# Second attention in two-step units with merged diagonal steps and VectorE masks; products issued in two parts in both attentions

## The reference

```python
xn = _layernorm(x)
s = _L0_attn_ref(xn, ...)              # full attention: softmax(q k / sqrt(8)) v, output matrix, residual
g = _silu(_L0_ffn_ref(xn, W_fc, W_proj))   # square(relu), then 5 steps of a spiking neuron
x = x + s * g
xn = _layernorm(x)
s = _L1_attn_ref(xn, ...)              # causal attention with a bias that is linear in the key's position
g = _silu(_L1_ffn_ref(xn, ...))        # 3 cycles of a small coupling network
x = x + s * g
```

```python
attn = attn + alibi
attn = jnp.where(causal, attn, jnp.finfo(x.dtype).min)
p = jax.nn.softmax(attn, axis=-1)
```

## Time and profile before

| | us |
|---|---|
| device time, median of 3 runs | 1046.53 (1045.78 to 1047.62) |
| device time of the profiled execution | 1043.26 |
| its span | 1041.5 |
| first attention, first to last exponential | 69.3 to 592.8 |
| middle | 597.6 to 681.0 |
| second attention, first to last exponential | 685.1 to 1026.7 |
| TensorE busy | 883.8 (85%) |
| ScalarE busy | 858.6 (82%) |
| VectorE busy | 439.0 (42%) |
| GpSimd busy | 122.6 (12%) |

### The profile page before, as it was taken

The page is one execution under the profiler, slowest core; times in us unless marked ns, Lnnn a source line. Parts: engine busy times, 40 slices in busy tenths (PEclk is TensorE's granted clock), DMA queues, the critical chain, the costliest instruction groups (busy, mean ns, idle before and its releaser), DMA issues. The chain is left out here.

```text
span 1041.5 us, 18319 instructions
## 1 busy us (share of the span) xinstructions
PE 883.8 (85%) x7078; PEld 337.8 (32%) x7078; DVE 439.0 (42%) x915; ACT 858.6 (82%) x1017; POOL 122.6 (12%) x135
## 2 busy tenths in 40 slices
PE   2757998799998999989999788768888899889886
PEld 1322333233333333323333242323333333334332
DVE  7522163443656426563265777802212411222222
ACT  5748999999999999999999756567878878887883
POOL 1001020130202302023020210000011002002001
PEclk9869999999999999999999999869999999999999
DMA  5862020100202002020000160100202202112000
GB/s 159 272 224 29 1 65 2 63 4 1 86 21 71 36 1 86 21 80 26 1 21 21 42 185 0 41 1 2 65 18 70 66 1 84 31 33 84 0 0 21
DMA packets 31950, 52.97 MB, mean 51 GB/s; under 512 B 5512, under 2 KB 16392, under 8 KB 31880
## 3 DMA queue, kind: packets, MB, share of 16 engines
q1 hardware_dynamic: 31880, 52.01, 16.1%
HBM read 31.29 MB, written 20.71 MB: 50 GB/s over the span
## 5 line engine op out<-in xcount | busy, mean ns | idle before, releaser
L921 ACT ACTIVATE a_probs<-a_sc 128x1024 f32<-128x1024 f32 x512 | 483.5, 1030 | 46.8 <-PE a_sc L1110 46.4
L1784 ACT ACTIVATE a_probs<-a_sc 128x1024 f32<-128x1024 f32 (+3 forms) x384 | 283.5, 819 | 55.3 <-PE a_sc L1912 50.3
L1124 PE MATMUL a_o<-a_probs,vt 128*18 128x512 f32 x2048 | 244.7, 595 | 0.0
L1110 PE MATMUL a_sc<-q_st,k_st 32*128 32x512 f32 x1024 | 130.6, 496 | 55.4 <-ACT a_probs L921 48.2
L1926 PE MATMUL a_o<-a_probs,a_v_st 128*16 128x512 f32 (+3 forms) x1536 | 163.2, 498 | 6.7 <-DVE a_o_sb L1857 6.7
L1110 PEld LDWEIGHTS a_sc<-q_st,k_st 32*128 32x128 f32 x1024 | 53.1, 183 | 215.2 <-ACT a_probs L921 201.2
L1906 PE MATMUL a_sc<-q_st,k_st 32*128 32x512 f32 (+3 forms) x768 | 87.7, 443 | 36.9 <-ACT a_probs L1784 30.2
L1857 DVE COPY a_o_sb<-a_o 128x512 f32<-128x512 f32 x32 | 22.1, 691 | 158.7 <-PE a_o L1926 158.7
L1906 PEld LDWEIGHTS a_sc<-q_st,k_st 32*128 32x128 f32 x768 | 39.8, 185 | 141.7 <-issue 98.4
L1124 PEld LDWEIGHTS a_o<-a_probs,vt 128*18 128x18 f32 x2048 | 47.4, 97 | 111.3 <-issue 72.0
L948 POOL TENSOR_TENSOR a_hidden<-a_hidden 128x512 f32<-128x512 f32 x32 | 38.4, 1200 | 158.5 <-DVE a_hidden L1048 158.5
(11 more groups left out here) (234 smaller groups left out, 827.1 us busy)
## 6 DMA issues: line engine op xcount, KB each, us to landing
q_st<-q_hl SPq DMA_DIRECT2D x48, 256.0 KB
k_st<-k_hl SPq DMA_DIRECT2D x48, 256.0 KB
q_hl<-parts SPq DMA_DIRECT2D x12, 512.0 KB, 3.4
k_hl<-parts SPq DMA_DIRECT2D x12, 512.0 KB, 4.0
q_hl<-p_parts SPq DMA_DIRECT2D x4, 512.0 KB, 3.9
k_hl<-p_parts SPq DMA_DIRECT2D x4, 512.0 KB, 4.7
out_dram<-x SPq DMA_DIRECT2D x8, 256.0 KB, 2.3
x<-in_L_attn_x_dram SPq DMA_DIRECT2D x3, 512.0 KB, 5.8
```

The lines of the kernel that those rows point to most:

```text
L921: nc.scalar.activation(probs[t % RING][:, 2 * pair:2 * pair + 2, :], scores[unit % SLOTS][:, :, :], ACT.Exp).then_inc(expd, 1)
L1110: ins = nc.tensor.matmul(scores[(2 * t + i // 2) % SLOTS][:, i % 2, :], k_st[part, g, kt * P:(kt + 1) * P], q_st[part, g, qh * HALF:(qh + ...
L1124: ins = nc.tensor.matmul(o_ps[32 * h:32 * h + 2 * W9, :], vt[b % 2][:, kt, gp, h, W9 * gs:W9 * gs + 2 * W9], probs[t % RING][:, h, :], sta ...
L1784: nc.scalar.activation(probs[j % PR][:, 2 * pair:2 * pair + 2, 0:HALF - q0], scores[unit % SC][:, :, 0:HALF - q0], ACT.Exp).then_inc(exp_d ...
```

## The change

- First attention: product(t) takes a range of columns. For an odd step the last 256 queries are issued one pair later, between score(2p) and the side piece; the even step and the first 256 queries of the odd one stay after score(2p+1).
- Second attention, new in the manner of the first: steps in pairs, `LAG1` 2, `RING` 4, two groups share one bank `o_ps` (18 columns of values per head), the same 32x32 transposes on VectorE at each of the now 4 ends of a sequence. Diagonal blocks are three steps instead of four: width 512, widths 384 and 128 side by side in one 512-wide step, width 256. So 40 steps a sequence, 160 in all, 320 exponentials. Products of odd steps are shared out as in the first attention (a merged step by its two blocks).
- Masks: group 0 (`STEEP` is 1) keeps the mask matmuls. The other three groups' probabilities are masked after the exponential on VectorE: min with 3e38 and times a 0/1 triangle, in place, 4 heads x 128 columns each; the product waits for it. A merged step has two masks.
- `turn_out` and `keep` are gone from the middle; the same transposes are side pieces `z` of the second attention with a copy on VectorE. Its gate is tanh on ScalarE and one VectorE operation. The last half's `mix` is done in two `tail` pieces with VectorE instead of GpSimd.
- The output matrix of layer 1 is loaded as `wo_x1` in eight small DMAs, issued between those of `wo_x` and that of `bo`. Two tiny activations load Gelu's and Exp's tables at the start and end of the middle. Values of two sequences are spread at once (`spread`).
- The second attention clears its semaphores at its end (`sem.wiped`).

```diff
-                by_slot = a["L0_attn_w_out"].rearrange("(g s j d) c -> s j d g c", g=2, s=2, j=G)
-                for s2 in range(2):
-                    for j in range(G):
-                        at = 32 * j + W9 * s2
-                        sp.dma_start(s["wo_x"][at:at + D, :, :], by_slot[s2, j]).then_inc(s["wo_in"], 16)
+                for name, slots, wait in (("L0_attn_w_out", s["wo_x"], s["wo_in"]), ("L1_attn_Wo", s["wo_x1"], s["w1_in"])):
+                    by_slot = a[name].rearrange("(g s j d) c -> s j d g c", g=2, s=2, j=G)
+                    for s2 in range(2):
+                        for j in range(G):
+                            at = 32 * j + W9 * s2
+                            sp.dma_start(slots[at:at + D, :, :], by_slot[s2, j]).then_inc(wait, 16)
...
-                        dve.wait_ge(s["w1_in"], 16 * 7)
+                        dve.wait_ge(s["w1_in"], 16 * (2 * G + 6))
+                        nc.vector.tensor_scalar_mul(s["wo_x1"][:, :, :], s["wo_x1"][:, :, :], 0.5)
+                        nc.vector.tensor_scalar_mul(s["bo"][:, 1, :], s["bo"][:, 1, :], 0.5)
...
-                def product(t):
+                def product(t, c0, c1):
                     b, gp, qh, gs, kt = place(t)
                     opens, closes = gs == 0 and kt == 0, gs == 1 and kt == BT - 1
-                    pe.wait_ge(expd, 2 * t + 2)
-                    if opens and t > 0:
-                        pe.wait_ge(o_free, t // STEP_END)
-                    if b > 0 and t % PER == 0:
-                        pe.wait_ge(side_in, fill_index("v0", b, 1) + 1)
+                    if c0 == 0:
+                        pe.wait_ge(expd, 2 * t + 2)
+                        if opens and t > 0:
+                            pe.wait_ge(o_free, t // STEP_END)
+                        if b > 0 and t % PER == 0:
+                            pe.wait_ge(side_in, fill_index("v0", b, 1) + 1)
                     for h in range(G):
-                        ins = nc.tensor.matmul(o_ps[32 * h:32 * h + 2 * W9, :], vt[b % 2][:, kt, gp, h, W9 * gs:W9 * gs + 2 * W9],
-                                               probs[t % RING][:, h, :], start=opens, stop=closes, tile_position=(0, 32 * h))
-                    ins.then_inc(pv_done, 1)
+                        ins = nc.tensor.matmul(o_ps[32 * h:32 * h + 2 * W9, c0:c1], vt[b % 2][:, kt, gp, h, W9 * gs:W9 * gs + 2 * W9],
+                                               probs[t % RING][:, h, c0:c1], start=opens, stop=closes and c1 == HALF, tile_position=(0, 32 * h))
+                    if c1 == HALF:
+                        ins.then_inc(pv_done, 1)
 
...
+                    if 0 <= 2 * pair - 1 - LAG < S:
+                        product(2 * pair - 1 - LAG, CUT, HALF)
                     for one in pieces_at(pair):
                         piece_of(*one)
                     if 2 * pair < S:
                         score(2 * pair + 1)
-                    for t in (2 * pair - LAG, 2 * pair + 1 - LAG):
-                        if 0 <= t < S:
-                            product(t)
+                    if 0 <= 2 * pair - LAG < S:
+                        product(2 * pair - LAG, 0, HALF)
+                        product(2 * pair + 1 - LAG, 0, CUT)
         sem.wiped()
...
+                nc.scalar.activation(warm[:, :], scalars[:, 0:2], ACT.Gelu)
...
-                keep(0, pa[:, 0:2, :])
                 couple(ROUNDS - 1, 0)
                 couple(ROUNDS - 1, 1)
-                keep(1, pb[:, 0:2, :])
-                keep(2, pb[:, 2:4, :])
-                keep(3, pa[:, 0:2, :])
+                nc.scalar.activation(warm[:, :], half_b[:, :], ACT.Exp)
 
...
+LAG1 = 2
+STEEP = 1
+
+
+def causal_steps():
+
+    steps = []
+    for gp in range(2):
+        for qh in range(2):
+            own = HT * qh
+            for gs in range(2):
+                blocks = [([(kt, 0, 0, HALF)], ()) for kt in range(own)]
+                blocks.append(([(own, 0, 0, HALF)], (0,)))
+                blocks.append(([(own + 1, P, 0, 3 * P), (own + 3, 3 * P, 3 * P, P)], (0, 3)))
+                blocks.append(([(own + 2, 2 * P, 0, 2 * P)], (0,)))
+                for n, (pieces, masked) in enumerate(blocks):
+                    opens, closes = gs == 0 and n == 0, gs == 1 and n == len(blocks) - 1
+                    steps.append((gp, qh, gs, pieces, masked, opens, closes))
+    return steps
+
+
...
+        if 0 < b < B:
+            fill("mix", b - 1, 1, 3, 4)
+        if b < B:
+            fill("z", b, 0, 5)
+            fill("z", b, 1, 6)
+            fill("mix", b, 0, 16, 17)
+        else:
+            fill("tail", b - 1, 0, 1)
+            fill("tail", b - 1, 1, 2)
...
+                for t in range(S):
+                    b, r = divmod(t, PER1)
+                    if t >= RING:
+                        act.wait_ge(pv_done, t - RING + 1)
+                    for pair in range(2):
+                        unit = 2 * t + pair
+                        act.wait_ge(scored, unit + 1)
+                        nc.scalar.activation(probs[t % RING][:, 2 * pair:2 * pair + 2, 0:width(t)],
+                                             scores[unit % SLOTS][:, :, 0:width(t)], ACT.Exp).then_inc(expd, 1)
...
+                def lift(e):
+                    b, k = divmod(e, ENDS)
+                    dve.wait_ge(pv_done, PER1 * b + closing[k] + 1)
+                    nc.vector.transpose(turn[e % 2][:, :], o_ps[:, :]).then_inc(o_free, 1)
+
+                def settle(e):
+                    t = turn[e % 2]
+                    used = t[:, :].rearrange("p (n r) -> p n r", r=32)[:, :, 0:2 * W9].rearrange("p n (s r) -> p n s r", r=W9)
+                    dve.wait_ge(o_free, e + 1)
+                    ends.after(nc.vector.reciprocal(recip[:, :, :], used[:, :, :, D]))
+                    ends.after(nc.vector.tensor_tensor(
+                        used, used, recip[:, :, :].rearrange("p n (s o) -> p n s o", o=1).broadcast_to([P, HALF // 32, 2, W9]), ALU.mult))
+                    nc.vector.transpose(on[e % ENDS][:, :], t[:, :]).then_inc(on_rdy, 1)
+
+                def mask(t):
+                    step = plan[t % PER1]
+                    if not late_mask(step):
+                        return
+                    dve.wait_ge(expd, 2 * t + 2)
+                    keep = tri[:, :].rearrange("p (o q) -> p o q", o=1).broadcast_to([P, G, P])
+                    for n in step[4]:
+                        part = probs[t % RING][:, :, n * P:(n + 1) * P]
+                        ins = nc.vector.scalar_tensor_tensor(part, part, LARGEST, keep, ALU.min, ALU.mult)
+                    ins.then_inc(masked, 1)
+
+                def gate(b, hf):
...
+                e = 0
+                for pair in range(LAST):
+                    b, r = divmod(pair, PER1 // 2)
+                    ending = e < B * ENDS and 2 * pair - LAG1 == PER1 * (e // ENDS) + closing[e % ENDS] + 1
+                    if ending:
+                        lift(e)
+                    if 0 <= 2 * pair - 1 < S:
+                        mask(2 * pair - 1)
+                    for n, kind, at, hf, piece, pieces in pieces_at(pair):
+                        if piece == pieces - 1 and kind != "tail":
+                            evacuate(n, kind, at, hf)
+                    if 2 * pair < S:
+                        mask(2 * pair)
+                    if ending:
+                        settle(e)
+                        e += 1
+                    for n, kind, at, hf, piece, pieces in pieces_at(pair):
+                        if kind == "tail":
+                            evacuate(n, kind, at, hf)
+                    for hf in range(2):
+                        if b < B and r == GATE_AT[hf]:
+                            gate(b, hf)
 
             @block.tensor
...
+                    for n, (kt, q0, at, w) in enumerate(pieces):
...
+                        if early:
+                            for i in range(G):
+                                ins = nc.tensor.matmul(banks[i][:, early[n] * P:(early[n] + 1) * P], s["ident_bf"][:, :],
+                                                       s["mask_kq"][:, :], start=False, stop=True)
+                                if i % 2 == 1 and n == len(pieces) - 1:
+                                    ins.then_inc(scored, 1)
...
+                def shares(t):
+
+                    pieces = plan[t % PER1][3]
+                    if t % 2 == 0:
+                        return pieces, []
+                    if len(pieces) == 2:
+                        return pieces[:1], pieces[1:]
+                    kt, q0, at, w = pieces[0]
+                    if w < HALF:
+                        return pieces, []
+                    return [(kt, 0, 0, CUT)], [(kt, CUT, CUT, HALF - CUT)]
+
+                def product(t, share):
+                    b, r = divmod(t, PER1)
+                    gp, qh, gs, _, _, opens, closes = plan[r]
+                    pieces = shares(t)[share]
```

(23 more changed lines are left out.)

406 lines of the change are left out of this document (163 added, 243 removed).

## The result

The changed kernel takes 982.41 us (median of 4 runs, 980.99 to 982.99) where the kernel before took 1046.88 on the same chip: ratio 0.9383, 95% interval 0.9367 to 0.9399. It is 64 us faster, 18 us more than the 46.7 of the forecast.

What follows compares the result with a forecast made beforehand. The prediction took ScalarE as the fullest engine, with its idle time nearly all ended by TensorE's scores. Gains of 12.5 (first attention), 27.5 (second), 3.1 (middle) and 3.6 (tail) sum to 46.7: 1046.53 to about 1000 us, range 974 to 1024.

Steps and rivals of the forecast that it cites:

- First attention, products in parts: First attention: splitting products evens TensorE's halves, pairs fall from 4.05 us to 3.95, 3.91 or 3.80; 18.5 us, less 1.7 for tanh.
- The lower case of a half product free of its start: First attention: if the half product pays no starting cost, heavy pairs take 3.83 us and the gain is 30.
- ScalarE alone binds: Rival, both attentions: TensorE's extra starts overlap, first attention at 3.80 a pair, second with 20 us idle; 970 us, chance 0.14.
- The cost at the start: Start of first attention: eight wo_x1 loads ahead of bo make VectorE, then TensorE, wait longer; 4.3 us lost.
- Exponentials: Second attention: 64 pairs of widths 384 and 128 become one full exponential each; 9.2 us gained.
- Idle time of the second attention: Second attention: ScalarE's idle time falls from 54.7 to 36.4 us, summed part by part; 18.3 us gained.
- late TensorE in the diagonal units: Second attention: halves of pairs around diagonal steps overrun, 0.8 us for each of 8 halves-of-heads; 6.4 us of idle time left.
- masks of group 0: Second attention: mask matmuls of 0.33 us, 8 a sequence, where TensorE is already late; 10.6 us of idle time left.
- Masks on VectorE: Second attention: masks moved to VectorE cost nothing, hidden because the product is due about 2.5 us after its exponential.
- The rival of small waits: Rival, second attention: VectorE finishes masks late, 0.3 us on each of 72 masked steps, 22 us; 1022 us, chance 0.19.
- The clock: Rival, second attention: fewer matmuls let TensorE's clock fall, full pairs take 5.1 us instead of 3.77; slower, chance 0.04.
- Middle and tail: Middle without turn_out and keep ends with VectorE, 3.1 us gained; stretch after the last exponential falls 12.0 to 8.4, 3.6 gained.

Runs made afterwards that it cites:

- experiment 7: The changed kernel with a second operation of the mask's kind and size, to spare tiles, ahead of each VectorE mask: 1004.46 us, ratio 0.9603.
- experiment 5: The changed kernel with whole products in the second attention, order and lag kept: 994.12 us, ratio 0.9502.
- experiment 6: The changed kernel with the diagonal steps unmerged (512, 384, 256, 128 columns), masks on VectorE, mixing pieces at units 19 and 20: 1062.26 us, ratio 1.0169.
- experiment 9: The changed kernel with unmerged diagonal steps (512, 384, 256, 128) and all masks on TensorE: 1069.06 us, ratio 1.0207.
- experiment 10: The changed kernel with unmerged diagonal steps in the order 512, 128, 384, 256, masks on VectorE: 1024.43 us, ratio 0.9794.
- experiment 12: The changed kernel with unmerged diagonal steps, all masks on TensorE, and one whole product behind each score: 1041.2 us, ratio 0.9974.
- experiment 2: The changed kernel with whole products in the first attention: 1004.26 us, ratio 0.9607.
- experiment 3: The changed kernel with the loads of bo ahead of the eight of wo_x1: 977.36 us, ratio 0.9348.
- experiment 4: The changed kernel with all masks on TensorE (STEEP 4), diagonal steps still merged: 1011.25 us, ratio 0.9668.
- experiment 8: The changed kernel with eight idle matmuls on TensorE at the end of the middle: 983.83 us, ratio 0.9409.
- experiment 11: The changed kernel with the loads of bo first and the scaling of wo_x and bo later on VectorE: 975.6 us, ratio 0.9332.
- experiment 1: The kernel before, with products of odd steps in two parts in the first attention only: 1023.28 us, ratio 0.9786.

## Why the prediction was right, and where its sizes were off

**First attention, products in parts: right, the size too small.** The mechanism and both halves of the pair came out to 0.01 us, and a unit with an fc piece takes 3.90 (forecast 3.91). Measured over 125 steady pairs: 3.883 us against 4.067 before, 23.0 us gained where the terms gave 16.8. Small terms make the 6: a pair before costs 4.067 on average, not the 4.05 of the one pair read (2.1 us); the eight tanh cost nothing, since ScalarE has slack wherever TensorE sets the pace (1.7); light pairs take 3.75, not 3.80, and heavy ones 3.93, not 3.95 (1.3 and 1.2). The lower case of a half product free of its start can be excluded, and so can the rival "ScalarE alone binds": heavy pairs that follow each other are TensorE's, at 3.93. A single one among light pairs costs ScalarE nothing, as the ten pairs from 161.03 on show.

**The cost at the start: right.** Forecast 4.3, measured 18.67 - 15.02 = 3.65 for the time from the first exponential to the thirteenth; issuing the loads in the other order gives 5 us by the medians and 3.7 by the ratios. The end of the wait came at 82.88, forecast 83.5.

**Exponentials: right**, 9.1 for 9.2 by ScalarE's busy time in the stage (the exponentials' own group goes from 283.5 to 275.0, 8.5). The 6.0 us worked out from the Trainium skill, ScalarE: Activation LUTs, section on what ACT_TABLE_LOAD costs, are less than this trace shows.

**Idle time of the second attention: the step that was off.** Forecast 36.4 left, 24.05 measured. Term by term, four sequences each: after half-width steps 5.1 (7.4); late TensorE in the diagonal units nothing (6.4), since ScalarE's timeline has no gap over 0.26 from 706 to 728 us, where diagonal units of the groups without TensorE's masks stand; masks of group 0 7.8 (10.6); side pieces 5.8 (4); start 3.5 (6); falls of the clock 0 (2). The remaining 1.8 I can't place. So the sum by halves of a pair was too strict: the forecast counted each late half as lost. The halves seem to borrow from each other, since the three units of the ring let scores run up to a step and a half ahead of ScalarE, and a half that is 0.38 late costs nothing when the next is early. The stretches without gaps fit this; no run changes the ring to show it.

**Masks on VectorE: right.** 0.69 us each, and 2.9 us of waits. Experiment 7 shows how far the margin goes: one more operation of 0.69 is free at most steps and not where masks, a gate and an end meet, once a sequence. The rival of small waits needs that doubling to come about; it then reaches its 22 us, but in the main by a few long waits and the clock that falls at three of them, not by 0.3 on each of 72 steps.

**The clock: did not fall in the second attention once it was up**, PEclk is 0.98 there and 1.00 after its start. But the rival's mechanism is real and was rated on the wrong cause. Taking matmuls away does not do it: experiment 5 has the masks gone as well, and no falls. The falls stand in the four kernels with unmerged steps (experiments 6, 9, 10 and 12), with TensorE's masks or without, and in experiment 7 at a wait for a mask; with merged steps and timely masks there is none between the start and the last exponential. By the Trainium skill, TensorE: Matmul & The Clock Gate, section Part 1, the clock follows how busy TensorE has been; the traces agree in that a stall of TensorE stands at or just ahead of the three falls in experiment 7. A stall alone does not decide it: in experiment 7's last sequence two of 1.03 and 1.00 us bring none, and the changed kernel keeps PEclk 1.00 through a longer one:

```profile
721.51 0.51 PE L1926 MATMUL a_sc<-q_st,k_st 32*128 32x512 f32 x4 [1.31 <-ACT a_probs L1804]
```

**Middle and tail: the steps held, and the lower clock, which these terms left out, took about half.** The middle gave 1.2, not 3.1. The second attention does start behind VectorE's twist, which ends at 661.46. But the twist's end came 1.9 us later behind the first attention than before, and 1.4 of them stand in one place, where four matmuls run at PEclk 0.58. Before and after:

```profile
624.53 1.98 PE L1522 MATMUL n_ps<-y,cn_w 128*128 128x512 f32 x4
...
606.46 3.35 PE L1538 MATMUL n_ps<-y,cn_w 128*128 128x512 f32 x4
```

This belongs to the execution and not to the kernel. Twelve profiled executions have this middle; in eight, those of experiments 2, 3, 4, 5, 7, 8, 11 and 12, these matmuls take 1.98 and the middle 89.1 to 89.5 us, which is the forecast's gain of 3.1 within 0.3. In the other four it takes 90.8 to 91.1.

The tail gave 1.35, not 3.6. To the last addition it is 10.1 us, where the forecast had 8.4: it counted one output piece of 1.1 us, where two follow each other, at 1.69 and 2.08, with VectorE between them. Both run partly or wholly at the lower clock (PEclk 0.70 and 0.50 in their stretches). In experiment 5, where the clock stays up, they take 1.13 and 1.16, and the same stretch 8.6 us; there VectorE's passes are short enough to make up for the second piece.

```profile
971.77 1.69 PE L1985 MATMUL a_side<-wo_x,on 128*128 128x128 f32 x8 [2.56 <-DVE on L1847]
...
973.98 2.08 PE L1985 MATMUL a_side<-wo_x,on 128*128 128x128 f32 x8 [0.52 <-DVE a_mix L1878]
```

**What the parts are worth together.** Undone one at a time in the changed kernel, by the medians: the first attention's parts 22 us, the second's 12, masks 29, merging 80. The last three sum to 121 where the stage gained 40. They are not separate gains: units of two steps with a lag of two make narrow steps dear (experiment 9 is 46 us slower than experiment 1, though its second attention has parts and experiment 1's has not), and merging pays that back. Of these 46 us, 28 are the order of scores and products (experiment 12); how the rest divides between the shorter lag and the clock stays open. The forecast's term for merging, 9.2 for the exponentials, was right as a difference between the two kernels, and would have been wrong by 70 us as the worth of the edit.

## What to carry to other kernels

Where an engine alternates between feeding the bottleneck and clearing up behind it, the clearing up of a wide step must not stand against the work of a narrow one: pair or merge steps so that each unit gives the bottleneck the same amount, before anything else is split finer. Move work that stands between a score and its exponential to another engine even when that engine is not faster; its place in the chain is what it costs. And read who waits behind the first wait of an instruction stream before adding loads to a queue.

## What the runs showed of the hardware

- The clock kept its upper level in a stage that gave TensorE less to do. In experiment 5 it was busy 219.7 of 290 us in the second attention at PEclk 1.00, with every mask but group 0's gone from it; in experiment 6 it was busy 292.6 of 378.5 at 0.84.

```profile
690.00:980.00 290.00, 219.73 (x2384) 90.93 (x2388) 105.46 (x168) 259.51 (x307) 20.53 (x18) 1.00 0.13 42
```

- One wait can be dear: in experiment 7 a stall of TensorE of about 1 us is followed in three of four sequences by 7, 10 and 20 us at 1.2 GHz, in which ScalarE works 46%, 61% and 72% of the time. In the fourth it is not, and neither is one of 1.31 us in the changed kernel; what makes the difference stays open.
- Eight dummy matmuls just before a stage held the full clock through an idle stretch of 2.9 us and for 2.5 us of the stage, and then it fell all the same, for 13.2 us (experiment 8).
- The same instructions can meet either level in different executions: four matmuls of the middle took 1.98 us in eight profiled executions and 3.35 to 3.68 in four, which moved the end of the middle by some 1.6 us.
